# Two groups ahead of the top layer's parts, and the contexts' low halves one block later, in a three-layer interaction kernel

## The chip, the cores and the metric

The kernel runs on one core of one Trainium2 chip. The metric is the device time in microseconds of one execution; the time quoted is the median of 3 runs.

## What is computed

A batch of 512 samples looks up 39 embedding rows of 16 numbers each. Three interaction layers follow, then two dense layers and a last product. Cut to what matters here:

```python
def _cin_layer(X0, Xi, W, b):            # W: (128, 39*Fi), X0: (512, 39, 16)
    Wr = W.reshape(H, F0_, Fi)
    return jnp.einsum('hjk,bjd,bkd->bhd', Wr, X0, Xi) + b[None, :, None]
Xi = X0
for W, b in [(W0, b0), (W1, b1), (W2, b2)]:
    Xi = _cin_layer(X0, Xi, W, b)
    res.append(Xi.sum(axis=2))
z = jnp.concatenate(res, axis=1)
h = jnp.concatenate([z, dense_ctx], axis=1)
h = jnp.maximum(h @ W_top1 + b_top1, 0.0)
h = jnp.maximum(h @ W_top2 + b_top2, 0.0)
y = h @ W_top3
```

Of the third interaction layer only the sum over the 16 positions is wanted. So it is computed from sums over positions of (first-layer input) times (second-layer output), which the program calls g, with one product with W2 for each of the 39 fields. This is "the top layer" of the text.

## The kernel before, in words

**Tiling.** The 512 samples times 16 positions are 8192 columns, cut into 16 chunks of 512 columns; a chunk has 4 blocks (i = 0 to 3) of 128 columns. In each block the 39 fields of the second layer are taken in 10 groups (g = 0 to 9) of four fields, the last of three. PE (TensorE) makes three matmuls per group (`layer1`, line 704): the 32-bit operands are split into a high and a low half, and high by high, high by low and low by high are added in one PSUM bank.

**Who drains the groups.** Groups 1, 4, 6 and 9 go to one of two banks `d_ps`, and DVE (VectorE) scales and adds them field by field (`add_group`, line 551, 15 fields a block). Groups 0, 2, 3, 5, 7 and 8 go to one of three banks `a_ps`; ACT (ScalarE) scales them into `parts` (`stage`, line 930), and POOL (GpSimd) adds them in four adds a block (line 311), the first two into `parts`, the last two into `left`. DVE then reduces `left` to `x2t` (`reduce_parts`, line 563), in the next block after its group 4, and PE multiplies `x2t` by `diag` into `g_ps` (`g_block`, line 745). ACT copies `g_ps` to `g_sb` and `z` (`store_g`, lines 939 and 940).

**Order.** There is no scheduler. Each engine runs a list written by hand: tables of places (i, position in the block) say behind which group of `layer1` on PE, of `add_group` on DVE or of `stage` on ACT another step stands. A place of PE counts groups g, one of DVE its own groups d = 0 to 3 (fields groups 1, 4, 6, 9), one of ACT its own a = 0 to 5 (groups 0, 2, 3, 5, 7, 8). Semaphores hold an engine where its data are not ready.

**The steps that the change touches.** `layer2(part)` (line 758) is the top layer: 39 products into the upper half of `quad_ps`. Part 0 takes chunks 0 to 7 and stands in chunk 8 (256 columns), part 1 takes chunks 8 to 11 and stands in chunk 15, the last one (128 columns); both stand ahead of the group at LAYER2_AT. Part 2, behind all chunks, isn't moved. A part waits for `g_stored` of the last block it uses: for part 0 that is the last block of chunk 7, whose product PE makes behind group 1 of block 1 of chunk 8, directly ahead of the part. ACT stores a part's sums with `store_z3` (line 945) behind its group at STORE_Z3_AT.

In the last chunk ACT copies the dense contexts and their weights with rounding to the high half (lines 981 and 982), and DVE takes from them the low halves (lines 601 and 604), behind its group at LOW_CTX_AT. PE needs them behind the last chunk, for the first products of the dense layers (line 852), ahead of which it also waits for DVE's and ACT's last groups.

```python
if d >= D_RING:
    pe.wait_ge(vector_added, NDF * q + D_ENDS[d - D_RING])
```

This wait holds PE ahead of group 6 of a block until DVE has taken its first group (d = 0), and ahead of group 9 until it has taken its second (d = 1). An add of POOL into `left` (k = 2) waits for the `x2t` of the block before, since `left` has one buffer.

Of the kernel before, what the change touches and what calls it, by code (L numbers as in the profile page):

```python
# [76 lines left out]
LATE_L0_AT = {(1, 7): 0, (2, 0): 1, (2, 1): 2, (2, 3): 3, (2, 5): 4, (3, 0): 5, (3, 2): 6}  # L77
TRANSPOSE_AT, LATE_TRANSPOSE_AT = (0, 9), (1, 2)
STORE_XT_AT, LATE_STORE_XT_AT = (1, 0), (1, 2)
LAYER2_AT, STORE_Z3_AT = (1, 2), (1, 1)  # L80

G_AT, STORE_G_AT = {(1, 9): 0, (2, 9): 1, (3, 9): 2}, {(1, 5): 0, (2, 5): 1, (3, 5): 2}
LAST_G_AT, STORE_LAST_G_AT = (1, 1), (1, 0)
REDUCE_AT, FIRST_REDUCE_AT = 1, 2

CLEAR_CTX_AT, HIGH_CTX_AT, LOW_CTX_AT = (0, 2), (2, 2), (2, 3)
HIGH_X1_AT, LOW_X1_AT, SUM_X1_AT, BIAS_Z1_AT = (3, 0), (3, 1), (0, 0), (1, 2)
PART_HIGH_X1_AT, PART_LOW_X1_AT = (3, 2), (3, 2)
LATE_HIGH_X1_AT, LATE_LOW_X1_AT = (3, 2), (3, 2)
# [1012 lines left out]
```

## Time and profile before

| | |
|---|---|
| median of 3 runs | 669.59 us (668.69 to 670.15) |
| the profiled execution, its own time | 670.7 us |
| its span | 668.9 us |
| mean granted clock of PE | 0.995 of full |
| PE busy | 644.9 us, 96% of the span |
| DVE, ACT, POOL busy | 458.9, 480.0 and 497.0 us |
| the chain that ended last, share of PE | 94% |
| second-layer matmuls (line 704) on that chain | 40% into a_ps and 25% into d_ps |

A share of busy time is an average over the span; where PE is at 96%, what is left for a change of order are the few places at which PE stands, and the head and the end of the program. Rows with a start and a duration are in microseconds from the span's start. The listed end of a matmul is modelled, and the next one starts before it, so distances are taken from start to start.

### The profile page before, as it was taken

The page shows a single profiled execution, that of the slowest core. Times are in us where ns is not written, and L with a number is a line of the kernel's source. Part 1 is how long each engine was busy: PE and PEld are TensorE (multiplying, and loading weights), DVE is VectorE, ACT ScalarE, POOL GpSimd, SP SyncE. Part 2 cuts the span into 40 slices and gives each one's busy share as a digit, 9 for nine tenths or more (in the row PEclk, how much of TensorE's full clock was granted, in tenths as well). Part 3 has the DMA queues.
Part 4 walks back from the last instruction along what each step waited for, and adds up shares of the span by engine and source line. Part 5 has one row for each costly group of instructions (what it writes and reads, how often), then busy time and mean ns, then how long its engine had stood idle before and what let it go on. Part 6 is the DMA issues. An engine that isn't in the chain of part 4 may idle for free.

```text
span 668.9 us, 11234 instructions
## 1 busy us (share of the span) xinstructions
PE 644.9 (96%) x2676; PEld 479.0 (72%) x2676; DVE 458.9 (69%) x1183; ACT 480.0 (72%) x1737; POOL 497.0 (74%) x467
## 2 busy tenths in 40 slices
PE   3599999999999999999999999999999999999998
PEld 1387677777777777777787777777776777779773
DVE  1367777778686968777725786868687877774920
ACT  1457678878787879697815787878796978784912
POOL 5779888979797988888835797979888886553710
PEclk9989999999999999999999999999999999999999
DMA  6643515151514233251500514132241404002000
GB/s 159 140 100 80 124 26 118 36 120 13 128 27 102 54 75 79 44 111 34 119 11 2 119 13 108 25 81 51 46 85 28 103 10 118 4 4 93 2 0 1
DMA packets 68264, 43.32 MB, mean 65 GB/s; under 512 B 49483, under 2 KB 61710, under 8 KB 66458
## 3 DMA queue, kind: packets, MB, share of 16 engines
q1 hardware_dynamic: 56870, 38.04, 25.4%
q0 software_dynamic: 5184, 1.29, 2.3%
q10 hardware_dynamic: 6158, 3.45, 2.0%
q8 instruction: 15, 0.25, 0.2%
q14 instruction: 37, 0.30, 0.1%
HBM read 39.58 MB, written 1.96 MB: 62 GB/s over the span
## 4 chain that ended last, share of the span: by engine, by line
PE 94%; issue 2%; DVE 1%; DMA 1%; ACT 1%; ACTq 0%; POOLq 0%; POOL 0%; DVEq 0%
PE a_ps L704 40%; PE d_ps L704 25%; PE quad_ps L655 14%; PE quad_ps L758 5%; PE g_ps L745 5%; PE g_ps L814 1%; DMA g_sb<-w_dram 1%; PE quad_ps L672 1%; PE a_ps L871 1%; PE quad_ps L659 1%; PE d_ps L842 1%; ACT parts L930 0%; DVE parts L551 0%; DVE x2t L563 0%; PE a_ps L842 0%
## 5 line engine op out<-in xcount | busy, mean ns | idle before, releaser
L930 ACT ACTIVATE parts<-a_ps,xt 128x128 f32<-128x128 f32 x1536 | 424.1, 383 | 129.7 <-PE a_ps L704 115.3
L551 DVE SCALAR_TENSOR_TENSOR parts<-d_ps,xt,parts 128x128 f32<-128x128 f32 x704 | 201.7, 343 | 108.9 <-PE d_ps L704 98.9
L311 POOL TENSOR_TENSOR parts<-parts 128x512 f32<-128x512 f32 x128 | 163.5, 1293 | 99.3 <-ACT parts L930 98.0
L704 PE MATMUL a_ps<-w_hi,x_hi 128*128 128x512 f32 x384 | 181.3, 472 | 1.5 <-issue 1.5
L311 POOL TENSOR_TENSOR left<-parts 128x512 f32<-128x512 f32 x128 | 167.3, 1323 | 7.5 <-ACT parts L930 5.9
L285 POOL DMA_INDIRECT emb<-tables_dram,rows_now x150 | 144.0, 960 | 25.3 <-issue 18.5
L704 PE MATMUL a_ps<-w_hi,x_lo 128*128 128x512 f32 x384 | 152.4, 397 | 0.6 <-issue 0.6
L704 PE MATMUL a_ps<-w_lo,x_hi 128*128 128x512 f32 x384 | 151.4, 394 | 0.0
L704 PE MATMUL d_ps<-w_hi,x_hi 128*128 128x512 f32 (+1 forms) x256 | 127.0, 496 | 0.9 <-DVE parts L551 0.9
L655 PE MATMUL quad_ps<-products,w_sb 117*128 117x512 f32 (+1 forms) x210 | 107.4, 592 | 0.0
L704 PE MATMUL d_ps<-w_lo,x_hi 128*128 128x512 f32 (+1 forms) x256 | 97.8, 382 | 0.6 <-ACT xt L908 0.6
L704 PE MATMUL d_ps<-w_hi,x_lo 128*128 128x512 f32 (+1 forms) x256 | 97.5, 381 | 0.0
L563 DVE TENSOR_REDUCE x2t<-left 128x128 f32<-128x1280 f32 x64 | 94.6, 1478 | 2.0 <-POOL left L311 1.5
L704 PEld LDWEIGHTS a_ps<-w_hi,x_hi 128*128 128x128 f32 x384 | 72.6, 189 | 27.1 <-issue 9.4
L704 PEld LDWEIGHTS a_ps<-w_lo,x_hi 128*128 128x128 f32 x384 | 72.7, 189 | 24.5 <-issue 7.9
L704 PEld LDWEIGHTS a_ps<-w_hi,x_lo 128*128 128x128 f32 x384 | 72.3, 188 | 18.7 <-issue 1.1
L494 DVE TENSOR_TENSOR products<-shifted,rows_ps 117x512 f32<-117x512 f32 x105 | 70.2, 682 | 3.1 <-ACT rows_ps L918 3.1
L704 PEld LDWEIGHTS d_ps<-w_hi,x_hi 128*128 128x128 f32 x256 | 48.3, 189 | 28.0 <-issue 12.1
L704 PEld LDWEIGHTS d_ps<-w_lo,x_hi 128*128 128x128 f32 x256 | 48.6, 190 | 25.7 <-issue 17.1
L704 PEld LDWEIGHTS d_ps<-w_hi,x_lo 128*128 128x128 f32 x256 | 48.3, 189 | 8.6
L551 DVE SCALAR_TENSOR_TENSOR parts<-d_ps,xt,b_rows 128x128 f32<-128x128 f32 x64 | 22.4, 349 | 36.4 <-PE d_ps L704 31.0
L655 PEld LDWEIGHTS quad_ps<-products,w_sb 117*128 117x128 f32 (+1 forms) x210 | 39.8, 190 | 9.2
(72 smaller groups left out, 428.4 us busy)
## 6 DMA issues: line engine op xcount, KB each, us to landing
shifted<-x_rows SPq DMA_DIRECT2D x45, 312.0 KB
shifted<-x_rows SPq DMA_DIRECT2D x45, 234.0 KB
diag<-xt SPq DMA_DIRECT2D x240, 4.9 KB
rows<-x_rows SPq DMA_DIRECT2D x45, 78.0 KB
emb<-tables_dram,rows_now POOLq DMA_INDIRECT x150
w_sb<-w_dram SPq DMA_DIRECT2D x6, 384.0 KB
shifted<-x_first SPq DMA_DIRECT2D x12, 136.5 KB
g_sb<-w_dram ACTq DMA_DIRECT2D x2, 768.0 KB
```

Source lines behind the costliest of these rows:

```text
L285: nc.gpsimd.indirect_dma_start(out=emb[0:parts, buf, g, :], out_offset=None, in_=tables[:, :], in_offset=bass.IndirectOffsetOnAxis(ap=rows ...
L311: nc.gpsimd.tensor_tensor(to, parts[:, i % 2, now:now + GF, :], parts[:, i % 2, more:more + GF, :], ALU.add).then_inc(pool_added, 1)
L494: nc.vector.tensor_tensor(products[0:PK, t, :], shifted[0:PK, t, :], rows_ps[0:PK, :], ALU.mult).then_inc(products_ready, 1)
L551: nc.vector.scalar_tensor_tensor(now, d_ps[d % D_RING][:, H * at:H * (at + 1)], xt[:, u, i, j:j + 1], before, ALU.mult, ALU.add).then_inc( ...
L563: nc.vector.tensor_reduce(x2t[:, i % 2, :], left[:, :, :], AX_X, ALU.add).then_inc(x2t_ready, 1)
L655: nc.tensor.matmul(quad_ps[:, :], w0_sb[0:rows, t, :], products[0:rows, t, :], start=(t == 0), stop=(t == QT - 1)).then_inc(products_used, 1)
L659: return nc.tensor.transpose(bank[:, FIELDS * i:FIELDS * (i + 1)], rows3[0:FIELDS, 128 * i:128 * (i + 1)], ident[:, :])
L672: mm = nc.tensor.matmul(quad_ps[:, cols], w0_sb[0:rows, t, :], products[0:rows, t, cols], start=(t == 0), stop=(t == QT - 1))
L704: return nc.tensor.matmul(bank[:, 0:H * len(fields)], x[:, u, 128 * i:128 * (i + 1)], w[:, fields[0]:fields[-1] + 1, :].rearrange("p j h - ...
L745: nc.tensor.matmul(g_ps[:, 0:(FIELDS + 1) * BLK_B], x2t[:, i % 2, :], diag[:, i, :, :].rearrange("p b j -> p (b j)"), start=True, stop=Tru ...
L758: mm = nc.tensor.matmul(z3_ps[:, 0:(c1 - c0) * CB], w2_sb[:, j, :], g_sb[:, j, c0 * CB - base:c1 * CB - base], start=(j == 0), stop=(j == ...
L930: last = nc.scalar.activation(parts[:, i % 2, 2 + GF * a + at, :], a_ps[(NA * i + a) % A_RING][:, H * at:H * (at + 1)], ACT.Copy, scale=xt ...
```

## The change

LAYER2_AT goes from (1, 2) to (1, 4): in chunks 8 and 15 the groups 2 and 3 of block 1 stand ahead of the part instead of behind it. STORE_Z3_AT goes from (1, 1) to (1, 2): ACT stores the part's sums one of its groups later. LOW_CTX_AT goes from (2, 3) to (3, 0): in the last chunk DVE makes the low halves behind the first group of block 3 instead of behind the last of block 2. No instruction is added or removed, and POOL's and SP's lists are the same.

```diff
-LAYER2_AT, STORE_Z3_AT = (1, 2), (1, 1)
+LAYER2_AT, STORE_Z3_AT = (1, 4), (1, 2)
...
-CLEAR_CTX_AT, HIGH_CTX_AT, LOW_CTX_AT = (0, 2), (2, 2), (2, 3)
+CLEAR_CTX_AT, HIGH_CTX_AT, LOW_CTX_AT = (0, 2), (2, 2), (3, 0)
```

PE in chunk 8, block 1, with what each instruction waits for (`a_ps` are the groups 2 and 3, `quad_ps` the top layer's part):

```order
 L745 MATMUL g_ps<-diag,x2t 128x320 [waits x2t_ready]
+L704 MATMUL a_ps<-w_hi,x_hi 128x512 [waits staged_ready]
+L704 MATMUL a_ps<-w_lo,x_hi 128x512
+L704 MATMUL a_ps<-w_hi,x_lo 128x512
+L704 MATMUL a_ps<-w_hi,x_hi 128x512 [waits staged_ready]
+L704 MATMUL a_ps<-w_lo,x_hi 128x512
+L704 MATMUL a_ps<-w_hi,x_lo 128x512
 L758 MATMUL quad_ps<-g_sb,w_sb 128x256 [waits late_loaded,g_stored,xt_ready]
 L758 MATMUL quad_ps<-g_sb,w_sb 128x256 x38
```

Six matmuls now stand between the product into `g_ps` and the part that waits for ACT's copies of it; in chunk 15 the same six move, ahead of a part that waits for `z3_stored` and for a `g_stored` of chunk 11.

DVE in chunk 15, from the end of block 2 (`left`) to the second group of block 3; 601 and 604 are the contexts' low halves:

```order
 L551 SCALAR_TENSOR_TENSOR left<-d_ps,xt,parts 128x128 [waits vector_added]
+L551 SCALAR_TENSOR_TENSOR parts<-d_ps,xt,b_rows 128x128 [waits x2t_ready,d_filled]
+L551 SCALAR_TENSOR_TENSOR parts<-d_ps,xt,no_bias 128x128
+L551 SCALAR_TENSOR_TENSOR parts<-d_ps,xt,parts 128x128 [waits vector_added] x2
 L601 TENSOR_TENSOR x_hi<-shifted,x_hi 16x512 [waits ctx_hi_ready]
 L604 TENSOR_TENSOR x_lo<-shifted,x_lo 16x512
```

The four instructions of block 3's first group, which free PE's bank for group 6, now stand ahead of the two low halves.

## Rows read from the trace of the kernel before

**Rows 1.** Page, part 1: busy time, share of the span, instructions of PE

```profile
PE 644.9 (96%) x2676; PEld 479.0 (72%) x2676; DVE 458.9 (69%) x1183; ACT 480.0 (72%) x1737; POOL 497.0 (74%) x467
```

**Rows 2.** Waits of PE, whole span: waiting line, releaser, us in total, times, longest

```profile
PE d_ps L704 <- DVE parts L551: 0.9, 1, 0.9
PE quad_ps L758 <- issue: 0.7, 1, 0.7
```

**Rows 3.** Timeline, chunk 8 around part 0, PE and ACT: start, duration, engine, line

```profile
336.37 0.70 PE L745 MATMUL g_ps<-diag,x2t 128*128 128x320 f32 x2
337.78 17.07 PE L758 MATMUL quad_ps<-g_sb,w_sb 128*128 128x256 f32 x78 [0.70 <-issue]
...
337.43 0.25 ACT L940 COPY z<-g_ps 128x8 f32<-128x8 f32 x1
```

**Rows 4.** Chain that ended last, behind part 0: start, duration, piece

```profile
354.85 1.40 PE a_ps L704 x6
```

**Rows 5.** Timeline, chunk 15 around part 1, PE

```profile
605.62 0.70 PE L745 MATMUL g_ps<-diag,x2t 128*128 128x320 f32 x2
606.16 8.87 PE L758 MATMUL quad_ps<-g_sb,w_sb 128*128 128x128 f32 x78
```

**Rows 6.** Timeline, DVE, end of chunk 15

```profile
628.98 1.50 DVE L601 TENSOR_TENSOR x_hi<-shifted,x_hi 16x512 fp32r<-16x512 f32 x1
630.49 1.70 DVE L604 TENSOR_TENSOR x_lo<-shifted,x_lo 16x512 fp32r<-16x512 f32 x1
...
634.30 1.48 DVE L563 TENSOR_REDUCE x2t<-left 128x128 f32<-128x1280 f32 x1
635.69 1.37 DVE L551 SCALAR_TENSOR_TENSOR parts<-d_ps,xt,parts 128x128 f32<-128x128 f32 x5
636.98 0.70 DVE L551 SCALAR_TENSOR_TENSOR left<-d_ps,xt,parts 128x128 f32<-128x128 f32 x2
639.20 1.49 DVE L563 TENSOR_REDUCE x2t<-left 128x128 f32<-128x1280 f32 x1 [1.51 <-POOL left L311]
```

**Rows 7.** Chain that ended last, the first group of block 3 on DVE

```profile
632.22 1.14 DVE parts L551 x4
```

**Rows 8.** Timeline, PE, blocks 3 and the first dense products

```profile
629.32 0.39 PE L704 MATMUL d_ps<-w_hi,x_lo 128*128 128x512 f32 x1
...
632.12 0.40 PE L704 MATMUL a_ps<-w_hi,x_lo 128*128 128x512 f32 x1
633.40 0.50 PE L704 MATMUL d_ps<-w_hi,x_hi 128*128 128x512 f32 x1 [0.88 <-DVE parts L551]
...
635.60 0.34 PE L704 MATMUL d_ps<-w_hi,x_hi 128*128 128x384 f32 x1
...
637.74 0.50 PE L852 MATMUL d_ps<-x_hi,x_lo 80*128 80x512 f32 x1
...
640.83 0.78 PE L745 MATMUL g_ps<-diag,x2t 128*128 128x320 f32 x2 [0.40 <-DVE x2t L563]
```

**Rows 9.** Timeline, POOL, end of chunk 15

```profile
628.63 3.01 POOL L311 TENSOR_TENSOR left<-parts 128x512 f32<-128x512 f32 x2
632.87 2.53 POOL L311 TENSOR_TENSOR parts<-parts 128x512 f32<-128x512 f32 x2 [1.23 <-ACT parts L930]
636.47 2.53 POOL L311 TENSOR_TENSOR left<-parts 128x512 f32<-128x512 f32 x2 [1.06 <-ACT parts L930]
```

**Rows 10.** The same from 630 us: the second add of the first pair

```profile
629.89 1.75 POOL L311 TENSOR_TENSOR left<-parts 128x512 f32<-128x512 f32 x1
```

**Rows 11.** Timeline, ACT, the groups of block 3

```profile
629.52 4.29 ACT L930 ACTIVATE parts<-a_ps,xt 128x128 f32<-128x128 f32 x16
635.10 2.18 ACT L930 ACTIVATE parts<-a_ps,xt 128x128 f32<-128x128 f32 x8 [1.28 <-PE a_ps L704]
```

**Rows 12.** Groups by form: DVE subtractions of two SBUF tensors, busy us, mean ns

```profile
L620 DVE TENSOR_TENSOR w_lo<-g_sb,w_hi 128x1536 fp32r<-128x1536 f32 x2 | 3.5, 1755 | 2.3 <-issue 2.3
L620 DVE TENSOR_TENSOR w_lo<-g_sb,w_hi 128x1920 fp32r<-128x1920 f32 x1 | 2.2, 2151 | 0.0
```

## The prediction

> **What bounds the kernel.** I read the shares first: PE is busy 644.9 of 668.9 us [rows 1], so a change of order can only give back time in which PE stands. The waits of PE say where that is: behind the program's head it stands three times, 0.9 us for DVE ahead of a group, 0.7 us ahead of the top layer, and 0.4 us ahead of the last product into g_ps [rows 2, 8]. The timeline places them: the 0.7 us in chunk 8 [rows 3], the other two in the last block and at the last block's product, both in chunk 15's end [rows 8]. The change touches exactly these places.
>
> **Part 0 of the top layer (chunk 8).** The product into g_ps starts at 336.37 and the part at 337.78, 1.41 us apart [rows 3]. In chunk 15 the same pair stands 0.54 us apart with no wait listed [rows 5]. So PE really stands 1.41 − 0.54 = 0.87 us (the listed 0.70 counts from a modelled end). The row says "issue", but ACT's second copy of that product ends at 337.43 + 0.25 = 337.68, 0.10 us ahead of the part's start [rows 3], and the part waits for it (g_stored). The change puts two groups in between, 1.40 us for their six matmuls [rows 4]: they start at 336.37 + 0.54 = 336.91 and the part could start at 338.31. ACT's copies don't depend on these groups, so the part is released at about 337.78 as before, 0.53 us early. The groups' own waits are open (they want banks that ACT emptied in the block before and a group earlier). Term: **−0.87 us**.
>
> What is late next: nothing that I can see. Behind the part, PE goes straight to group 4, for DVE, which waits there as before. ACT has staged groups 2 and 3 while the part ran, stands in the storing of the sums until the part ends, and has group 5 next, so it is further ahead than before; POOL too. SP's and POOL's lists are unchanged. The storing one group later is hidden: PE asks for it only ahead of group 9.
>
> **Part 1 (chunk 15).** The part starts 0.54 us behind the product [rows 5]; its g_stored belongs to chunk 11. PE doesn't stand, so two groups in between give **0**.
>
> **Low halves (end of chunk 15).** All times here are on the clock of before. DVE ran 601 and 604 from 628.98 to 632.19, 1.50 and 1.70 us [rows 6], and only then the first group of block 3, 1.14 us to 633.36 [rows 7]. PE had finished group 5 with the matmul of 632.12 [rows 8]; matmuls of this form follow at 1.40 / 6 = 0.23 us [rows 4], so group 6 was due at 632.35 and began at 633.40: **1.05 us** of standing.
>
> What do the two instructions cost alone? 1,536 elements take 1.755 us and 1,920 take 2.151 [rows 12], which is 1.03 ns an element; from the nearer row, 512 elements come to 1.755 − 1024 × 0.00103 = 0.70 us, and I take the same for 16 partitions as for 128. 1.50 and 1.70 are thus stretched. POOL's rows say by what: its pair of adds from 628.63 took 3.01 us where an undisturbed pair takes 2.53 [rows 9], and of these 1.75 are the second add [rows 10]. Taken one after the other it closes: add one to 629.89, 601 runs to 630.48, add two to 629.89 + 1.75 = 631.64, 604 runs 0.55 us to 632.19. Each running alone has 0.55 to 0.60 us of DVE.
>
> The Trainium skill states such a rule (SBUF — State Buffer, SBUF: two separate sides): a DVE instruction with two SBUF inputs and a GpSimd instruction take one pair of ports in turn, each for its whole length. By it the stretch belongs to the place and the sum is the 1.94 us below; without it, it would be the first rival's. The rows above agree, with 3.01 against 2.53 us.
>
> New order: the first group's bank is full at 629.32 + 0.39 = 629.71 [rows 8], so DVE does it from about 629.75 to 630.89 (1.14 us, [rows 7]). POOL's pair is now undisturbed and ends at 628.63 + 2.53 = 631.16 [rows 9]. 601 then runs to about 631.75 and 604 to 632.32; POOL's next add starts at 632.87, when ACT has staged for it [rows 9], so they fit between. Lower bound of the two together: 1.1 us (none held); upper: 3.2 as in [rows 6].
>
> From there: PE passes group 6 at 632.35 without standing. Group 9 began at 635.60 [rows 8] and is due 1.05 us earlier, at 634.55; it needs DVE's second group. Eight instructions took 634.30 − 632.22 = 2.08 us from start to start [rows 6, 7], so this group of four is through at 632.35 + 1.04 = 633.39: open. ACT starts group 7's staging 1.05 us earlier, at 634.05 instead of 635.10, just behind its earlier work, which ends at 629.52 + 4.29 = 633.81 [rows 11]. It has group 7 ready at 635.2 and group 8 at 634.05 + 2.18 = 636.23, before POOL wants it. But POOL's first two adds end at 632.87 + 2.53 = 635.40 [rows 9], so its last pair starts there instead of at 636.47, ends at 637.93 instead of 639.00, and the last reduce starts at 638.13 instead of 639.20 [rows 6]. That is **−1.07 us** for the last product into g_ps, 639.76 instead of 640.83 [rows 8].
>
> Does PE get there in time? DVE's reduce of block 2 runs from 633.40; its seven last instructions took 637.68 − 635.69 = 1.99 us and start 1.39 us behind the reduce [rows 6], so they end at 636.8. The second dense product waits for that: 636.84 instead of 637.74. From there PE was busy to 640.83 − 0.40 = 640.43, a modelled end [rows 8], 2.69 us, so it is done at 639.53, ahead of 639.76. Behind it everything hangs on PE, so the end moves by the same. Term: **−1.07 us**.
>
> **Sum.** −0.87 − 1.07 = −1.94 us. The profiled execution took 670.7 us (span 668.9), 1.1 above the median; its waits stand for the others', so 670.7 goes to 668.8 and the median from 669.59 to 667.65, say **667.7 us**. That is −0.29%; a measurement of this kernel can tell about 0.2%, 1.34 us, from no change, so "faster" needs less than 668.25.
>
> **Rivals.** First, **the low halves cost 1.50 and 1.70 us wherever they stand.** For: one row each, 16 partitions, no other of that form. Then they run to 630.89 + 3.20 = 634.09, DVE's second group to 635.1 (group 9 starts at 635.2 instead of 635.60), the reduce of block 2 to 636.6, its last group to 638.5, and the second dense product waits till 638.57 instead of 637.74. PE is at the last product 2.69 us later, less the 0.17 by which a modelled end is late in chunk 8 (0.87 against 0.70), at 641.1 instead of 640.83: +0.27, and with part 0 −0.60, **669.0 us**. Against: POOL's 3.01 us.
>
> Second, **part 0 gives nothing** (the 0.87 us is a delay of PE's own at entering the part): −1.07 alone, **668.5 us**. For: the row says "issue". Against: the 0.10 us behind ACT's copy, and part 1 without such a delay.
>
> Third, slower: **the low halves collide with POOL's first pair of block 3.** If 604 isn't running when POOL starts at 632.87, it waits for an add (to 634.14) and ends at 634.72; the chain of the first rival then ends 0.6 later, +0.9 at the end, which eats part 0's gain: 669.6. If POOL makes both adds ahead of it (635.40), +2.2 and in sum +1.3, **670.9 us**. It decides where 601 starts later than some 632.3, 1.1 us later than I have it. For: a margin of 0.55 us between 604's end and POOL. Against: ACT's staging, which releases POOL, isn't moved.
>
> **Chances.** Forecast 0.65, first rival 0.17, second 0.10, third 0.04; 0.04 is left for what I don't see. The forecast's own range is 667.0 to 668.4: the unknown price of the low halves (1.1 to 1.4) is covered by POOL's pair and moves nothing, and runs scatter by 0.7 about their median. With the first and second rival the range is 667.0 to 669.1. Faster by over 0.2%: nine tenths of the forecast and a quarter of the second rival, 0.61. Slower by over 0.2%: 0.05. Within: 0.34.
>
> **What would show it.** In chunk 8 the part follows group 3 without a wait, and PE's 0.7 us entry is gone. Lines 601 and 604 take about 0.9 (part of it waiting for POOL) and 0.6 us; PE's wait ahead of group 6 is gone; POOL's last pair starts directly behind its first; the last reduce starts 1.07 us earlier relative to block 3. Wrong it is if 601 and 604 still take 3.2 us in sum, if a new wait shows on group 9, on the product of block 2 or on the second dense product, or if the part in chunk 8 still has a wait.

## The result, and the profile after

The changed kernel takes 667.63 us (median of 22 runs, 666.19 to 669.07), the kernel before 669.55 us (22 runs, 668.34 to 670.61): ratio 0.9971, 95% interval 0.9964 to 0.9978, that is 1.9 us less. The profiled execution took 667.98 us with a span of 666.2.

The waits of PE behind the program's head, which were 0.9, 0.7 and 0.4 us [rows 2, 8], are gone. Behind 80 us the list names no wait of PE any more; in the head these stay, and three others between the first and the second line shown (5.0, 1.1 and 0.9 us; columns: who waited, for what, us in total, times, longest):

```profile
PE g_ps L814 <- DMA g_sb<-w_dram: 10.9, 1, 10.9
...
PE d_ps L704 <- ACT xt L908: 0.6, 1, 0.6
PE a_ps L704 <- DVE x_lo L520: 0.6, 1, 0.6
PE a_ps L704 <- issue: 0.6, 1, 0.6
```

Chunk 8, timeline of PE and ACT after; it answers to [rows 3, 4]:

```profile
335.72 0.70 PE L745 MATMUL g_ps<-diag,x2t 128*128 128x320 f32 x2
336.02 0.64 PE L704 MATMUL a_ps<-w_hi,x_hi 128*128 128x512 f32 x1
...
337.41 0.39 PE L704 MATMUL a_ps<-w_hi,x_lo 128*128 128x512 f32 x1
337.64 17.00 PE L758 MATMUL quad_ps<-g_sb,w_sb 128*128 128x256 f32 x78
354.29 0.58 PE L704 MATMUL d_ps<-w_hi,x_hi 128*128 128x512 f32 x1
...
336.78 0.26 ACT L940 COPY z<-g_ps 128x8 f32<-128x8 f32 x1
337.15 2.18 ACT L930 ACTIVATE parts<-a_ps,xt 128x128 f32<-128x128 f32 x8
```

ACT's last copy of the sums ends at 337.04, 1.32 us behind the product's start as before, and the part now comes to it 0.60 us later, at 337.64, with nothing to wait for. ACT stages groups 2 and 3 (eight instructions) while the part runs.

The end of chunk 15 on DVE, POOL and ACT after; it answers to [rows 6, 7, 9, 11]:

```profile
628.12 0.35 DVE L551 SCALAR_TENSOR_TENSOR parts<-d_ps,xt,b_rows 128x128 f32<-128x128 f32 x1 [0.80 <-PE d_ps L704]
...
629.28 0.83 DVE L601 TENSOR_TENSOR x_hi<-shifted,x_hi 16x512 fp32r<-16x512 f32 x1
630.12 0.68 DVE L604 TENSOR_TENSOR x_lo<-shifted,x_lo 16x512 fp32r<-16x512 f32 x1
630.84 1.13 DVE L551 SCALAR_TENSOR_TENSOR parts<-d_ps,xt,parts 128x128 f32<-128x128 f32 x4
...
636.48 1.49 DVE L563 TENSOR_REDUCE x2t<-left 128x128 f32<-128x1280 f32 x1 [1.22 <-POOL left L311]
...
627.00 2.57 POOL L311 TENSOR_TENSOR left<-parts 128x512 f32<-128x512 f32 x2
631.25 2.55 POOL L311 TENSOR_TENSOR parts<-parts 128x512 f32<-128x512 f32 x2 [1.68 <-ACT parts L930]
633.75 2.53 POOL L311 TENSOR_TENSOR left<-parts 128x512 f32<-128x512 f32 x2
...
627.89 6.61 ACT L930 ACTIVATE parts<-a_ps,xt 128x128 f32<-128x128 f32 x24
```

DVE now waits 0.80 us for the first group of block 3, makes it, and the low halves take 0.83 and 0.68 us instead of 1.50 and 1.70. POOL's pair beside them is back at 2.57 us from 3.01. POOL's four adds of block 3 run without the pause of 1.06 us [rows 9], and ACT stages all six groups in one run of 24 instructions instead of 16 and 8 with 1.28 us between [rows 11].

PE at the last products, against [rows 8] (852 are the first dense products, 745 the products into g_ps):

```profile
633.41 0.81 PE L745 MATMUL g_ps<-diag,x2t 128*128 128x320 f32 x2
633.81 0.64 PE L852 MATMUL rows_ps<-x_hi,x_lo 80*128 80x512 f32 x1
635.32 0.50 PE L852 MATMUL d_ps<-x_hi,x_lo 80*128 80x512 f32 x1
...
637.20 0.79 PE L852 MATMUL a_ps<-x_hi,x_lo 80*128 80x512 f32 x1
638.11 0.78 PE L745 MATMUL g_ps<-diag,x2t 128*128 128x320 f32 x2
```

The list counts from modelled ends, so short stands don't show in it; the starts tell them. The last product into g_ps starts 0.91 us behind the matmul of line 852 ahead of it (637.20 to 638.11), where 0.63 is enough when nothing holds it (639.55 to 640.18, in the trace of experiment 4 with the low halves later still):

```profile
639.55 0.79 PE L852 MATMUL a_ps<-x_hi,x_lo 80*128 80x512 f32 x1
640.18 0.70 PE L745 MATMUL g_ps<-diag,x2t 128*128 128x320 f32 x2
```

So PE still stands 0.28 us there, for the last reduce, which ends at 636.48 + 1.49 = 637.97. Before, the same distance was 1.20 us (639.63 to 640.83).

The spans of two executions differ for reasons of their own, so each step is measured inside its trace, as a distance between starts on PE. "Product" here is one into g_ps (line 745). "A" runs in chunk 8 from the product ahead of the part to the first product behind it, "M" from there to the product ahead of the part in chunk 15, "B" from there to the first product behind that part, "C" from the same start as B to the last product into g_ps. "Start" is where A begins in the span. The profiled executions of all kernels of this study:

| kernel | start | A | M | B | C | median, ratio to before |
|---|---|---|---|---|---|---|
| before | 336.37 | 24.59 | 244.66 | 14.66 | 35.21 | 669.55 |
| the change | 335.72 | 23.63 | 244.65 | 14.65 | 34.11 | 667.63, 0.9971 |
| parts only | 335.41 | 23.62 | 244.61 | 14.65 | 35.21 | 668.56, 0.998 |
| low halves only | 334.86 | 24.60 | 245.23 | 14.66 | 34.10 | 668.65, 0.9978 |
| low halves later still | 335.25 | 23.62 | 244.69 | 14.65 | 36.62 | 670.54, 1.0016 |
| high halves from PSUM | 337.08 | 24.58 | 244.91 | 14.66 | 35.50 | 671.94, one run |
| parts one group on | 335.91 | 23.89 | 244.60 | 14.64 | 35.19 | 669.46, one run |
| low halves of 8 columns | 334.79 | 23.63 | 245.25 | 14.65 | 34.09 | 667.04, 0.9953 |
| sums stored one place earlier | 335.67 | 23.62 | 244.60 | 14.64 | 34.11 | 667.88, one run |

The ratios are those on record, each against the kernel before in the same set of runs (median 669.55, 669.68 or 669.82 us); they are not quotients of two medians and can differ from these by some 0.0007.

The change takes 0.96 us in A, nothing in M and B, and 1.10 us in C: 2.06 us. The two spans differ by 2.7 us, and 0.65 us of that lies ahead of A, where the two programs are the same; the medians differ by 1.92.

### The profile page after: what moved, and what is told of

Its sections match the earlier page's. It is cut to its first block, busy times and chain, and to the rows that moved or that the text cites. A ratio compares the mean times of both kernels' runs of the same rounds, so it can differ in the third digit from the quotient of the medians.

```text
span 666.2 us, 11234 instructions
## 1 busy us (share of the span) xinstructions
PE 644.0 (97%) x2676; PEld 478.7 (72%) x2676; DVE 457.2 (69%) x1183; ACT 480.6 (72%) x1737; POOL 497.3 (75%) x467
## 3 DMA queue, kind: packets, MB, share of 16 engines
q0 software_dynamic: 5184, 1.29, 2.3%
## 4 chain that ended last, share of the span: by engine, by line
PE 94%; DMA 3%; SPq 1%; DVE 1%; ACT 1%; issue 1%; POOL 0%; ACTq 0%
PE a_ps L704 40%; PE d_ps L704 25%; PE quad_ps L655 14%; PE g_ps L745 5%; PE quad_ps L758 5%; PE a_ps L871 1%; PE quad_ps L672 1%; DMA rows<-x_first 1%; DMA emb<-tables_dram,rows 1%; PE quad_ps L659 1%; PE d_ps L842 1%; DMA x_first<-emb 1%; DMA picks_sb<-picks_dram 1%; PE rows_ps L842 0%; PE a_ps L842 0%
```

## Experiment 1: the two edits apart

Parts only:

```diff
-LAYER2_AT, STORE_Z3_AT = (1, 2), (1, 1)
+LAYER2_AT, STORE_Z3_AT = (1, 4), (1, 2)
```

> The kernel before with the top layer's parts behind group 3 and their sums stored one place later; the low halves stay behind block 2. My theory (the two terms add up, each has one cause): PE goes from the product into g_ps to the part in chunk 8 over two groups in 1.9 us without a wait, 0.87 us are gained there (0.97 by the trace of the full change), nothing in chunk 15; the wait of 0.9 us ahead of group 6 and the 0.4 us ahead of the last product stay, lines 601 and 604 still take 1.5 and 1.7 us. Time 0.9 us less than before, ratio 0.9987. Rival (the gain comes from the low halves alone and the 0.87 us is an entry cost of the part): ratio 1.000, and a wait ahead of the part in chunk 8.

Measured: 668.56 us (10 runs) against 669.68 for the kernel before in the same set (27 runs), ratio 0.998, interval 0.9967 to 0.9993. A is 23.62, the part starts 1.91 us behind the product with no wait listed, C stays at 35.21, and 601 and 604 take 1.49 and 1.69 us. The waits of PE in its trace still hold the two of the end, and none for a part:

```profile
PE d_ps L704 <- DVE parts L551: 0.9, 1, 0.9
...
PE g_ps L745 <- DVE x2t L563: 0.4, 1, 0.4
```

Low halves only:

```diff
-CLEAR_CTX_AT, HIGH_CTX_AT, LOW_CTX_AT = (0, 2), (2, 2), (2, 3)
+CLEAR_CTX_AT, HIGH_CTX_AT, LOW_CTX_AT = (0, 2), (2, 2), (3, 0)
```

> The kernel before with the low halves behind the first group of block 3 and nothing else. My theory: 1.07 us less than before, ratio 0.9984; lines 601 and 604 together 1.5 us, no wait ahead of group 6, POOL's last pair directly behind its first. In chunk 8 the distance from the product to the part stays 1.41 us. Rival (the two edits need each other: the low halves fit only because POOL is further ahead behind the moved part in chunk 15): lines 601 and 604 stay at 3.2 us in sum and the time is 0.3 us more than before, ratio 1.0004.

Measured: 668.65 us (12 runs), ratio 0.9978, interval 0.9966 to 0.999. The product and the part in chunk 8 stay 1.41 us apart and A at 24.60, C is 34.10, and the two instructions and POOL read as after the full change:

```profile
630.00 0.81 DVE L601 TENSOR_TENSOR x_hi<-shifted,x_hi 16x512 fp32r<-16x512 f32 x1
630.82 0.68 DVE L604 TENSOR_TENSOR x_lo<-shifted,x_lo 16x512 fp32r<-16x512 f32 x1
...
627.70 2.56 POOL L311 TENSOR_TENSOR left<-parts 128x512 f32<-128x512 f32 x2
631.93 2.54 POOL L311 TENSOR_TENSOR parts<-parts 128x512 f32<-128x512 f32 x2 [1.67 <-ACT parts L930]
634.42 2.53 POOL L311 TENSOR_TENSOR left<-parts 128x512 f32<-128x512 f32 x2
```

So neither edit needs the other, and each of the rivals stated for these two runs falls. Both intervals lie below 1, but they are 0.0026 and 0.0024 wide, 1.7 and 1.6 us, which is more than either term; it is the distances A and C that separate them: 0.97 us for the parts (24.59 − 23.62) and 1.11 us for the low halves (35.21 − 34.10), and both together in the full change.

## Experiment 2: what the part in chunk 8 waited for

Against the forecast stood the rival that the 0.87 us were a cost of entering the part. One group in between, storing unmoved, tells: the wait would shrink, an entry cost would move along.

```diff
-LAYER2_AT, STORE_Z3_AT = (1, 2), (1, 1)
+LAYER2_AT, STORE_Z3_AT = (1, 3), (1, 1)
```

> The kernel before with the parts only one group on, behind group 2, and the storing unmoved. If PE waits for ACT's copy of the last sums (my theory), the copy still ends 1.31 us behind the product's start and the part can start 0.10 behind that, at 1.41 us; the product and the group take 0.54 + 0.70 = 1.24 us, so 0.17 us of the 0.87 stay: distance from the product to the part in chunk 8 1.41 us, as before. If the 0.87 us is an entry cost of the part behind any work (rival), the distance is 0.54 + 0.70 + 0.87 = 2.1 us.

Measured: the product starts at 335.91 and the part at 337.32, a distance of 1.41 us as expected, where an entry cost would have made 2.1. ACT's copy again ends 0.10 us ahead of the part:

```profile
335.91 0.70 PE L745 MATMUL g_ps<-diag,x2t 128*128 128x320 f32 x2
336.21 0.63 PE L704 MATMUL a_ps<-w_hi,x_hi 128*128 128x512 f32 x1
...
336.97 0.25 ACT L940 COPY z<-g_ps 128x8 f32<-128x8 f32 x1
...
337.32 17.07 PE L758 MATMUL quad_ps<-g_sb,w_sb 128*128 128x256 f32 x78
354.04 0.59 PE L704 MATMUL a_ps<-w_hi,x_hi 128*128 128x512 f32 x1
```

The traces also show that the part itself is longer where PE stood ahead of it: 16.72 us from its start to the next start (354.04 − 337.32, and 354.50 − 337.78 before), against 16.65 with the change (354.29 − 337.64). Those 0.07 us are most of what the gain in A is above 0.87. One group on gives 24.59 − 23.89 = 0.70 us, the group's length.

## Experiment 3: does the storing have to move along?

From the change, with the storing back at its old place:

```diff
-LAYER2_AT, STORE_Z3_AT = (1, 4), (1, 2)
+LAYER2_AT, STORE_Z3_AT = (1, 4), (1, 1)
```

> The change, with the storing of the part's sums left at its old place: ACT stores them behind its group 2, that is, stands there while the part runs, and stages group 3 only then. My theory (the storing one place on is hidden either way): PE has no new wait in chunks 8 and 15, since it wants group 3's bank again only at group 8, 2.1 us behind the part, and the time is that of the change within scatter. Rival (the storing had to move along): PE waits for ACT ahead of group 8 or later, 0.3 us or more in each of the two chunks.

Measured: 667.88 us in one run, A, B and C as with the change to 0.01 us, and no wait of PE behind 80 us. ACT's timeline in chunk 8 shows it standing in the storing with only group 2 staged, then storing, then staging groups 3 and 5 in one run, without PE missing a bank:

```profile
337.10 1.14 ACT L930 ACTIVATE parts<-a_ps,xt 128x128 f32<-128x128 f32 x4
354.62 0.47 ACT L945 ACTIVATE z<-quad_ps,bias2d 128x256 f32<-128x256 f32 x1 [16.39 <-PE quad_ps L758]
355.00 2.17 ACT L930 ACTIVATE parts<-a_ps,xt 128x128 f32<-128x128 f32 x8
```

The margin was wider than my expectation had it: group 8 starts 2.96 us behind group 4 (354.24 to 357.20), not 2.1, and one group's staging takes 1.14 us. By this one trace, the storing's place is worth nothing here.

## Experiment 4: why the low halves were slow

The forecast rests on one reading of two rows: 601 and 604 are short instructions that wait for POOL's adds. Two runs test it from opposite sides. First, put them on purpose where POOL adds without a pause. From the change:

```diff
-CLEAR_CTX_AT, HIGH_CTX_AT, LOW_CTX_AT = (0, 2), (2, 2), (3, 0)
+CLEAR_CTX_AT, HIGH_CTX_AT, LOW_CTX_AT = (0, 2), (2, 2), (3, 1)
```

> The change, with the low halves one place later still, behind DVE's second group of block 3 and the reduce of block 2, where POOL adds without a pause. If a DVE subtraction of two SBUF tensors and an add of POOL run in turn, each whole (my theory): line 601 waits for POOL's second add and line 604 for its third, 1.4 to 1.9 us each and 3.2 to 3.6 in sum, POOL's four adds of block 3 take 1.1 us longer, DVE's last group ends 2.9 us later and the end comes 2.7 us later than with the change: ratio to before 1.001, about 670.3 us. If the two cost 0.7 us each wherever they stand (rival), the end comes only 0.4 us later than with the change, about 668.0 us, ratio 0.998.

Measured: 670.54 us (10 runs), ratio 1.0016, interval 1.0002 to 1.0029. DVE and POOL, end of chunk 15:

```profile
632.34 1.57 DVE L601 TENSOR_TENSOR x_hi<-shifted,x_hi 16x512 fp32r<-16x512 f32 x1
633.92 1.66 DVE L604 TENSOR_TENSOR x_lo<-shifted,x_lo 16x512 fp32r<-16x512 f32 x1
...
630.82 2.54 POOL L311 TENSOR_TENSOR parts<-parts 128x512 f32<-128x512 f32 x2 [1.67 <-ACT parts L930]
633.32 3.41 POOL L311 TENSOR_TENSOR left<-parts 128x512 f32<-128x512 f32 x2
```

POOL's last add by itself, in a view from 635.5 us:

```profile
635.00 1.73 POOL L311 TENSOR_TENSOR left<-parts 128x512 f32<-128x512 f32 x1
```

The two are long again, 3.23 us in sum, and POOL's pair beside them is 0.9 us longer than 2.53. Laid one after the other they fit the rows: 601 is issued at 632.34 during POOL's second add, which ends at 630.82 + 2.54 = 633.36, and runs 0.55 us to 633.91; POOL's third add runs from there to about 635.04, where the fourth is issued (635.00, and undisturbed adds overlap by 0.04 in the rows); 604 runs 0.54 us to 635.58, POOL's fourth add from there to 633.32 + 3.41 = 636.73. Each turn is somewhat shorter than the instruction alone: 0.54 to 0.55 us for a subtraction that takes 0.68 undisturbed, 1.13 and 1.15 us for an add that takes 1.25 from start to start. C is 36.62, 2.51 us more than with the change, where I expected 2.7; as two fixed costs of 0.7 it would have been 0.4, so that rival falls. A fixed 1.5 and 1.7 us wherever they stand would look the same here; against that stand their 0.83 and 0.68 us after the change. PE's waits name the path:

```profile
PE rows_ps L852 <- DVE x_lo L604: 2.1, 1, 2.1
...
PE d_ps L852 <- DVE left L551: 0.6, 1, 0.6
```

The first is one that my expectation left out: PE wants the low halves for the very first dense product. It sets nothing by itself, since the second wait, 2 us on, ends later.

Second, leave them at the place of the kernel before, but take one of the two SBUF inputs away. ACT copies the 16 rows of each high half to a free PSUM bank first, and the subtraction reads it there:

```diff
-                            nc.scalar.copy(wt1c_split, wt1c_sb).then_inc(ctx_hi_ready, 1)
+                            nc.scalar.copy(wt1c_split, wt1c_sb).then_inc(ctx_copied, 1)
+                            act.wait_ge(ctx_copied, 1)
+                            nc.scalar.copy(rows_ps[32:48, :], ctx_split[32:48, :].bitcast(F32))
+                            nc.scalar.copy(quad_ps[64:80, :], wt1c_split[64:80, :].bitcast(F32)).then_inc(ctx_hi_ready, 1)
...
-                            nc.vector.tensor_tensor(ctx_split[low, :], ctx_sb[low, :], ctx_split[low, :].bitcast(F32),
+                            nc.vector.tensor_tensor(ctx_split[low, :], ctx_sb[low, :], rows_ps[low, :],
...
-                            nc.vector.tensor_tensor(wt1c_split[low, :], wt1c_sb[low, :], wt1c_split[low, :].bitcast(F32),
+                            nc.vector.tensor_tensor(wt1c_split[low, :], wt1c_sb[low, :], quad_ps[low, :],
```

> The kernel before, with the low halves at their old place, but the high half that each subtraction reads comes from PSUM: ACT copies the 16 rows of each to two free banks first, two copies of 0.65 us more on ACT. One SBUF input per subtraction is left, as in line 494, whose 105 instructions keep to 0.68 us beside POOL. If the pair of SBUF inputs is what makes DVE and POOL take turns (my theory), lines 601 and 604 take 0.65 to 0.75 us each though POOL's adds run beside them, POOL's pair stays at 2.5 us, and PE's wait ahead of group 6 is gone. If the place, the 16 partitions or the output's type make them slow (rival), they stay at 1.5 and 1.7 us. The time isn't the question: ACT's extra 1.3 us push its staging, 668.5 to 670 us.

Measured in its trace (one line more in the file, so 601, 604 and 311 are 602, 605 and 312):

```profile
629.92 0.68 DVE L602 TENSOR_TENSOR x_hi<-shifted,rows_ps 16x512 fp32r<-16x512 f32 x1
630.61 0.69 DVE L605 TENSOR_TENSOR x_lo<-shifted,quad_ps 16x512 fp32r<-16x512 f32 x1
...
629.68 1.29 POOL L312 TENSOR_TENSOR parts<-parts 128x512 f32<-128x512 f32 x1 [2.07 <-ACT parts L931]
630.94 2.58 POOL L312 TENSOR_TENSOR left<-parts 128x512 f32<-128x512 f32 x2
```

Both run right beside POOL's adds, and neither side is stretched: 0.68 and 0.69 us, POOL 1.29 and 2.58. Same place, same 16 partitions, same output type; of the subtractions only the second SBUF input is gone. The wait ahead of group 6 is gone as well. So it was the stretch that made PE stand there, not the old order in itself: on the rows of before, 628.98 + 0.68 + 0.69 + 1.14 gives 631.49 us for the end of DVE's first group, ahead of the 632.35 at which group 6 was due (an estimate). The execution took 671.94 us, 2 us above what I gave: A begins 0.7 us later than before, with a wait of 2.3 us in the head that only this trace has, and ACT's longer list costs PE 0.38 us ahead of block 3 and 1.28 ahead of the last product. C is 35.50; as a version it is no use, as an answer it is clear.

Together these two runs show the cause that the forecast had inferred: these DVE subtractions with two SBUF inputs and POOL's adds take turns. The Trainium skill (SBUF — State Buffer, SBUF: two separate sides) has the pair of ports held for the whole instruction, against a GpSimd instruction that reads SBUF, as these adds do. The traces agree with the taking in turn; the turns that they show are some 0.1 us shorter than the instructions take alone.

## Experiment 5: what the low halves still cost

The two subtractions cut to 8 of 512 columns each, at the new place; the low halves of the other columns aren't computed:

```diff
-nc.vector.tensor_tensor(ctx_split[low, :], ctx_sb[low, :], ctx_split[low, :].bitcast(F32),
+nc.vector.tensor_tensor(ctx_split[low, 0:8], ctx_sb[low, 0:8], ctx_split[low, 0:8].bitcast(F32),
...
-nc.vector.tensor_tensor(wt1c_split[low, :], wt1c_sb[low, :], wt1c_split[low, :].bitcast(F32),
+nc.vector.tensor_tensor(wt1c_split[low, 0:8], wt1c_sb[low, 0:8], wt1c_split[low, 0:8].bitcast(F32),
```

> The change, with each of the two subtractions cut to 8 of its 512 columns; the other columns' low halves aren't computed. It asks what the low halves still cost at their new place. My theory: nothing but the wait of 0.12 us ahead of the last product and the last reduce, since POOL's four adds set it: 0 to 0.15 us less than the change, ratio to before 0.997. Rival (DVE's last group sets it too, through the second dense product): up to 0.6 us less, ratio 0.996.

Measured: C is 34.09 against 34.11. The last product now waits 0.53 us for the last reduce, and that for POOL, whose four adds run back to back as before:

```profile
630.89 2.54 POOL L311 TENSOR_TENSOR parts<-parts 128x512 f32<-128x512 f32 x2 [1.65 <-ACT parts L930]
633.39 2.54 POOL L311 TENSOR_TENSOR left<-parts 128x512 f32<-128x512 f32 x2
```

So at their new place the low halves cost 0.02 us of C at most; POOL's four adds set the last product alone. The median of its 4 runs, 667.04 us, and the ratio 0.9953 (0.9936 to 0.9971) look like 0.6 us less than the change, which the trace doesn't bear out: the interval overlaps that of the change, and 4 runs don't settle 0.6 us.

## Why the prediction was right, point by point

**Part 0, −0.87 us: right, measured −0.96.** The wait was for ACT's copy (experiment 2), the two groups cover it with time over, and no new wait came behind the part. The 0.09 that the sum lacked is 0.07 for the part, which runs shorter when PE hasn't stood ahead of it, and 0.02 for the two groups, which with the product take 1.92 us instead of the reckoned 1.94.

**Part 1, 0: right.** B is 14.65 against 14.66.

**Low halves, −1.07 us: right, measured −1.10.** Step by step: 601 took 0.83, of which the end of POOL's pair (627.00 + 2.57 = 629.57) left 0.54 to run, and 604 took 0.68 where I had counted 0.57 for it. The difference is hidden, as the prediction said of this price: POOL's adds of block 3 run 631.25 to 636.28 without a pause and release the last reduce. The 0.03 beyond 1.07 is POOL's: its last pair starts 2.50 us behind the first, not 2.53.

The path of PE had more give than the waits list shows. Counted from the product ahead of part 1, group 9 starts 1.16 us earlier than before (29.98 to 28.82), not 1.05: in the row after a stand the next matmul also comes 0.34 us later instead of 0.23 (633.40 to 633.74). Some of it is lost again. The product of block 2 starts 0.06 us behind DVE's reduce (631.88 + 1.47 = 633.35 to 633.41), and 0.24 us behind the matmul ahead of it where that was 0.17: a new short stand at one of the places that the prediction named as signs against it. The second dense product starts 0.06 us behind the end of DVE's last group, as it did before (637.68 to 637.74, now 635.26 to 635.32). From the same origin it comes 0.80 us earlier, where the prediction gave it 0.90 (636.84 for 637.74). It starts 1.51 us behind the first product of line 852, where it was 1.32; if the 0.46 us of the pair behind it (638.08 to 638.54 before) held here too, PE stood about 0.39 us before and stands 0.57 us now. None of this reached the end: PE was ready for the last product 0.28 us before the reduce released it, and the prediction had reckoned 0.23 (639.53 to 639.76).

**The sum, −1.94 us: measured 1.92 by the medians,** 667.63 for 667.7. By the distances it is 2.06; that the medians come so near is partly luck, since the interval alone is ±0.5 us.

**The rivals.** The first (1.50 and 1.70 us wherever they stand) fell with the profile after, 0.83 and 0.68 us; the run with one input in PSUM took 0.68 and 0.69 even at the old place. The second (part 0 gives nothing) fell with A and experiment 2. The third, the collision with POOL, didn't happen at the new place: 604 ended at 630.80, 0.45 us ahead of POOL's next pair, for the 0.55 reckoned. One place further on they do collide, and C is 1.41 us longer than before; the 0.9 and the 2.2 us of the prediction were put on a collision at the new place, so that run doesn't measure them. The window between POOL's pairs is narrow: one DVE group earlier C is 35.21, in the window 34.11, one later 36.62.

None of the versions run is shown to be better than the change. What they leave open at the end is the 0.28 us ahead of the last product, which POOL's four adds set; having these end earlier wasn't tried. The stand ahead of the second dense product sets nothing: in experiment 5 that product comes 0.61 us earlier, and C is the same.

## What to carry to other kernels

Where an instruction takes twice what its element count asks for, look at what the other engine's rows do in the same microsecond: if both are stretched and the sum closes when you lay them one after the other, the cost may belong to the place, and a run with the instruction elsewhere tells. Here a subtraction of two SBUF tensors beside POOL's adds was cured by a pause of POOL (0.83 and 0.68 us) and by one input in PSUM (0.68 and 0.69). And where PE waits for the engine that drains its last product, put that much independent work in between: here one group left 0.17 us of the wait (1.41 less 0.54 and 0.70), two left none; more than two wasn't tried. Last, a list without waits is no proof that the engine never stands: compare distances between starts with the same pair elsewhere.

## What the runs showed that I had not expected

The profiled executions scatter by 2.3 us (334.79 to 337.08) in where A begins, ahead of everything that was changed. Between the parts, M is 244.60 to 244.91 in seven of nine and 245.23 and 245.25 in two; in both of these PE waits once for a copy of `diag` there, for instance, in the trace with the low halves only:

```profile
PE d_ps L704 <- DMA diag<-xt: 0.3, 1, 0.3
```

Such a wait isn't in the trace of before or of the change between the parts. By starts it is the whole difference: up to that place the distances between products are those of the trace of before to 0.1 us, from there on they are 0.61 and 0.64 us longer. Neither of these two kernels differs from the one that it was made from anywhere between the parts (the low halves stand in chunk 15), so it comes from the execution and not from the edit; the trace with the parts one group on has such a wait too, but ahead of A. The 0.6 us of M is more than half of either term here: a single pair of spans couldn't have told one edit from none. What makes the copy late in some executions wasn't tried.
